# Linear attention: ScalarE weights the second expert rows, writes both norms and divides by the denominators; VectorE copies V with its bias

## The chip, the cores and the metric

The kernel runs on one core of a Trainium2 chip. Its time is device time in microseconds (us), the median of several executions: 1312.03 before the change, over 3 runs from 1311.81 to 1312.66. The core has a matrix engine (TensorE, PE in the profile, with its weight loads as PEld), three engines that work element by element (VectorE as DVE, ScalarE as ACT, GpSimd as POOL), and a queue that issues transfers (SyncE, SP). Each engine takes its instructions in the order in which they were written for it; semaphores order them against other engines.

## The reference

Six layers follow each other on x of 8 x 256 rows of 128 numbers: a feed-forward block with local attention, an attention with decay, the first block again, a mixture of experts, a linear attention, and the mixture of experts once more. The change is in the linear attention, and in how the experts' results before and behind it are added to x:

```
yr = sum over the two best experts of w[n] * expert(n)       # mixture: ys + yr
x = x + 0.5 * (ys + yr)
xn = (x - mean) * rsqrt(var + 1e-5) * ln_g + ln_b            # of x, itself layer-normed first
q, k, v = split(xn @ w_qkv + b_qkv)
k = k * sigmoid(xn @ w_gate + b_gate)
q, k = elu(q) + 1, elu(k) + 1
num = (q @ k.T * causal mask) @ v
den = sum(q * cumsum(k)) + 1e-6
x = x + num / den @ w_proj + b_proj
```

Behind it stands the norm of the next mixture of experts.

## The kernel before, in words

X holds all 2048 rows as 16 tiles of 128 x 128. The linear attention works in NCH = 4 chunks of CT = 4 tiles (512 rows, two sequences). There is no planner: each engine has a function (la_pe, la_act, la_dve, la_pool) in which the order of the work is written out by hand, and the engines meet at semaphores. The stage begins when the rows of the experts' results come back from memory: for each chunk one transfer into U (first expert) and one into uT (second expert), issued one after the other by SyncE (L2239). It ends with a barrier of all engines (phase_end), behind which the next mixture of experts picks its experts.

First half, by chunk c:
- VectorE, added(c): add_experts (L2149) adds weight times row for the first expert and then for the second, one scalar_tensor_tensor a tile, eight a chunk; moments (L2445, L2449) takes mean and variance. Then normed(c-1, 0) (L2455) writes (x - mean) * rs of the chunk before into U.
- GpSimd, power(c, 0) (L2548, L2550): rs = (a * var + b) to the power -1/2. Behind the four powers it adds the projection's bias to X (x_bias, L2555).
- TensorE, turned(c) (L2259): transposes the four tiles of U. ScalarE, normed(c) (L2382): copies the turned chunk to uT with the norm's gain and bias. TensorE, gate_proj(c) (L2266), k_proj, q_proj. ScalarE, gates(c) (L2387): the sigmoid.
- TensorE's written order there: turned(0), turned(1), gate_proj(0), k_proj(0), turned(2), gate_proj(1), q_proj(0), turned(3), gate_proj(2), gate_proj(3), v_proj(0). v_proj(0) waits for all four gates, since V and a gate share a bank.

Second half, a loop over i in which the engines are some chunks apart:
- ScalarE: o_out(i-1) (L2414) copies the turned output of chunk i-1 out of its bank; exps(i+1) (L2395 to L2401) for both feature maps; v_out(i+1) (L2407) copies V out; x_out(i-2) (L2418).
- VectorE: gated(i+1) (L2469), masked(i) (L2485), result(i-1) (L2511: adds the projected output to X, then takes the moments for the next norm), features(i+1) (L2474, L2477), divided(i) (L2492, L2498: the denominators; L2504: four tiles times 1/denominator into osb), normed(i-1, 1) (L2455 again, into U).
- GpSimd: v_bias(c) (L2560) adds V's bias in place; power(c, 1).
- TensorE: out_proj(i-1), x_turned(i-2) (L2332), sums(i) (waits for V with bias, and for x_new of chunk i-1, since the banks are used again), k_proj, v_proj, scores, q_proj, o_turn(i) (L2317), and at the end the logits of the next stage (L2339).

The last stage of the kernel (add_last on VectorE, scale_second on ScalarE, L2156, L2164, L2168) adds the experts' rows of the second mixture: ScalarE multiplies the second expert's rows by their weights in place, VectorE adds the first expert's rows tile by tile and the second's with one tensor_tensor for the whole chunk.

Of the kernel before, what the change touches and what calls it, by code (L numbers as in the profile page):

```python
# [126 lines left out]
def build(nc, a, out):  # L127
    with ExitStack() as ctx:
# [177 lines left out]
        ndr = sb("ndr", [P, 2, CT])  # L306

# [1824 lines left out]
        def sums(k0, c):  # L2132
            return 2 * NT + c * (CT + 1) if k0 else 2 * c * CT

        def wait_added(eng, k0, c):
            eng.wait_ge(s.x_sum, sums(k0, c) + (CT + 1 if k0 else 2 * CT))
# [4 lines left out]
        def add_experts(dve, k0, c):  # L2141

            dve.wait_ge((s.gat0, s.gat1, s.gat2, s.gat3)[c], 16 * 2 * (k0 + 1))
            dve.wait_ge(s.s_tmp, NCH * (k0 + 1))
            for n in range(2):
                for t in range(c * CT, (c + 1) * CT):
                    if n:
                        dve.wait_ge(s.x_sum, sums(k0, c) + t - c * CT + 1)
                    dve.scalar_tensor_tensor(X[:, t, :], gathered(n, c)[:, t - c * CT, :], wc[:, n, t:t + 1], X[:, t, :],  # L2149
                                             ALU.mult, ALU.add).then_inc(s.x_sum, 1)  # L2150

        def scale_second(act, c):
            act.wait_ge((s.gat0, s.gat1, s.gat2, s.gat3)[c], 16 * 4)
            for t in range(CT):
                g = gathered(1, c)[:, t, :]
                m = act.activation(g, g, ACT.Identity, scale=wc[:, 1, c * CT + t:c * CT + t + 1])  # L2156
            m.then_inc(s.x_scaled, 1)

        def add_last(dve, c):
            xc = X[:, c * CT:(c + 1) * CT, :]  # L2160
            dve.wait_ge((s.gat0, s.gat1, s.gat2, s.gat3)[c], 16 * 4)
            dve.wait_ge(s.s_tmp, NCH * 2)
# [3 lines left out]
            dve.wait_ge(s.x_scaled, c + 1)  # L2166
            dve.wait_ge(s.x_sum, sums(1, c) + CT)
# [85 lines left out]
        def la_pe(pe, ph):  # L2253
# [47 lines left out]
            def sums(c):  # L2301
                v_, w = vA[c % 2], D + 1
                pe.wait_ge(s.p_sum, NCH + c + 1)
# [75 lines left out]
        def la_act(act, ph):  # L2379
# [44 lines left out]
            normed(0)  # L2424
            for c in range(1, NCH):
                normed(c)
                gates(c - 1)
            gates(NCH - 1)
            act.preload_act_table(ACT.Exp)
            for i in range(-1, NCH + 2):  # L2430
                if has(i - 1):
                    o_out(i - 1)
                if has(i + 1):
                    exps(i + 1)
                    v_out(i + 1)
                if has(i - 2):
                    x_out(i - 2)
            phase_end(act, "act", ph)

        def la_dve(dve, ph):  # L2440
# [10 lines left out]

            def normed(c, k):
                dve.wait_ge(s.rs_ready, LA_RS + k * NCH + c + 1)
                for t in range(c * CT, (c + 1) * CT):
                    m = dve.tensor_scalar(U[:, t, :], X[:, t, :], mv[:, t, 0:1], rs[:, 1, t:t + 1],  # L2455
                                          ALU.subtract, ALU.mult)
                m.then_inc(s.ln_done, 1)
# [29 lines left out]
            def divided(c):  # L2487
# [174 lines left out]
```

## Time and profile before

| | |
|---|---|
| median of 3 runs | 1312.03 us |
| the profiled execution, own time | 1309.68 us |
| its span in the profile | 1307.8 us |
| PE busy | 1153.8 us, 88% |
| DVE busy | 915.5 us, 70% |
| ACT busy | 850.6 us, 65% |
| POOL busy | 789.2 us, 60% |
| mean granted TensorE clock | 0.961 of full speed |

Busy time is what an engine spends in instructions, added up over the span; it hides which engine is waited for at a given moment. The linear attention runs from 1077 us to some 1150 us of the span, 5 to 6% of it. In a timeline each row gives its start, its length, the engine, the source line, the operation, what it writes and reads, how many instructions were merged, and in brackets how long the engine had been idle and what ended that. X is the residual, U and uT the two buffers named above, mv the moments, rs the reciprocal deviations, osb (sm in the rows) the divided output.

### The profile page before, as it was taken

To read this page: it belongs to the slowest core of one execution; us is meant where nothing else is said; L and a number is where in the kernel's file an instruction comes from. 1 tells how busy PE (TensorE), PEld (TensorE's weight loads), DVE (VectorE), ACT (ScalarE), POOL (GpSimd) and SP (SyncE) were. 2 spreads that over 40 slices of the span, in tenths; PEclk is the share of its full clock that TensorE was granted. 3 is DMA by queue.
4 is the path that set the end of the run, shared out by engine and by line. 5 is a ranking of instruction groups with operands and counts; after the bars stand their busy time and mean duration, and the time that the engine had idled before them with its cause. 6 is when DMAs were issued, how large, how long until landed. Compare 5 with 4: busy or idle time off the path is not lost.

```text
span 1307.8 us, 36416 instructions
## 1 busy us (share of the span) xinstructions
PE 1153.8 (88%) x12703; PEld 865.5 (66%) x12704; DVE 915.5 (70%) x2475; ACT 850.6 (65%) x2476; POOL 789.2 (60%) x705
## 2 busy tenths in 40 slices
PE   5899898999888999979998989989979985779995
PEld 2576685777755666536766856768569873648985
DVE  6898678887765666769886698878754337774334
ACT  3899858999544455549998589994425543334554
POOL 5888438886456354168873488854377753237772
PEclk8999999999989999989999999999879996978998
DMA  7011100011000000000111000113157650025775
GB/s 222 22 25 28 29 9 20 22 27 26 21 11 3 4 3 3 3 1 18 26 26 29 17 10 22 26 26 93 45 143 220 202 157 26 1 81 160 230 199 154
DMA packets 69808, 78.21 MB, mean 60 GB/s; under 512 B 25094, under 2 KB 50501, under 8 KB 69509
## 3 DMA queue, kind: packets, MB, share of 16 engines
q1 hardware_dynamic: 64133, 64.70, 17.6%
q0 software_dynamic: 5504, 11.28, 3.5%
q8 instruction: 100, 1.64, 0.6%
q14 instruction: 71, 0.58, 0.2%
HBM read 54.60 MB, written 8.78 MB: 48 GB/s over the span
## 4 chain that ended last, share of the span: by engine, by line
PE 55%; DVE 12%; ACT 10%; DMA 8%; POOL 6%; issue 5%; POOLq 1%; SPq 1%; DVEq 0%; ACTq 0%
PE bank L916 5%; PE bank L1846 5%; ACT pB L795 4%; DMA arena<-arena 3%; PE bank L637 3%; PE bank L600 3%; DMA y_rows<-stg,inv_u 3%; PE bank L928 3%; PE bank L1515 3%; PE bank L559 3%; PE bank L545 3%; PE bank L612 3%; PE bank L1536 3%; PE bank L551 3%; POOL arena L2176 2%
## 5 line engine op out<-in xcount | busy, mean ns | idle before, releaser
L864 POOL TENSOR_TENSOR rn<-ss,mhalf 128x16 f32<-128x16 f32 x64 | 187.2, 2924 | 6.8
L2104 DVE SCALAR_TENSOR_TENSOR act_b<-bank,vec,gl 128x128 f32<-128x128 f32 x258 | 75.0, 345 | 133.0 <-ACT gl L1927 112.9
L1846 PE MATMUL bank<-arena 128*128 128x128 f32 x1032 | 135.5, 282 | 1.6 <-issue 1.6
L1846 PEld LDWEIGHTS bank<-arena 128*128 128x128 f32 x1032 | 126.1, 197 | 6.2 <-issue 5.3
L795 ACT ACTIVATE pA<-bank,nb,rn 128x128 f32<-128x128 f32 x256 | 113.5, 484 | 3.0 <-DVE nb L726 3.0
L795 ACT ACTIVATE pB<-bank,nb,rn 128x128 f32<-128x128 f32 x256 | 113.3, 478 | 1.7 <-DVE nb L726 1.7
L850 POOL TENSOR_TENSOR arena<-arena 128x512 f32<-128x512 f32 x64 | 81.5, 1274 | 46.0 <-DVE nb L726 34.9
L1927 ACT ACTIVATE gl<-bank,vec 128x128 f32<-128x128 f32 x258 | 76.0, 365 | 51.1 <-PE bank L1846 36.0
L857 POOL TENSOR_TENSOR arena<-arena 128x512 f32<-128x512 f32 x64 | 81.3, 1271 | 43.1 <-DVE arena L689 16.4
L1609 DVE TENSOR_REDUCE act_b<-bank 128x2 f32<-128x512 f32 x128 | 79.5, 684 | 39.6 <-PE bank L1491 39.6
L2182 POOL DMA_INDIRECT y_rows<-stg,inv_u x86 | 84.6, 983 | 35.0 <-issue 18.6
L2176 POOL DMA_INDIRECT arena<-u_rows,inv_u x86 | 84.0, 977 | 32.5 <-issue 22.5
L721 DVE TENSOR_REDUCE mx<-bank 128x4 f32<-128x512 f32 x128 | 82.4, 685 | 25.9 <-PE bank L600 25.9
L687 DVE TENSOR_TENSOR arena<-bank,arena 128x512 f32<-128x512 f32 x128 | 87.4, 683 | 13.9 <-ACT arena L762 12.8
L776 ACT ACTIVATE pT<-bank 128x512 f32<-128x512 f32 x128 | 77.2, 604 | 22.8 <-PE bank L612 19.8
L762 ACT ACTIVATE arena<-bank 128x512 f32<-128x512 f32 x128 | 78.3, 613 | 18.5 <-PE bank L545 9.5
L916 PE MATMUL bank<-hT,arena 128*128 128x256 f32 (+1 forms) x384 | 89.2, 382 | 0.0
L689 DVE TENSOR_TENSOR arena<-bank,arena 128x512 f32<-128x512 f32 x128 | 87.0, 680 | 0.0
L1079 POOL TENSOR_SCALAR rs<-mv 128x2 f32<-128x2 f32 x48 | 10.9, 226 | 125.6 <-DVE mv L978 125.6
L784 ACT ACTIVATE arena<-bank 128x512 f32<-128x512 f32 x128 | 78.6, 614 | 8.0 <-PE bank L567 4.8
L637 PE MATMUL bank<-pT,arena 128*64 128x64 f32 (+1 forms) x1536 | 71.9, 242 | 13.5 <-DMA arena<-arena 12.0
L1052 ACT ACTIVATE gl<-bank,vec 128x256 f32<-128x256 f32 (+1 forms) x96 | 45.3, 472 | 49.6 <-PE bank L916 49.2
(334 smaller groups left out, 3135.9 us busy)
## 6 DMA issues: line engine op xcount, KB each, us to landing
arena<-in_L_ffn_We SPq DMA_DIRECT2D x86, 384.0 KB, 4.3
arena<-arena SPq DMA_DIRECT2D x64, 128.0 KB, 2.3
arena<-in_L_ffn_We SPq DMA_DIRECT2D x3, 768.0 KB, 7.4
arena<-U SPq DMA_DIRECT2D x32, 64.0 KB
u_rows<-U SPq DMA_DIRECT2D x2, 1024.0 KB, 5.2
U<-y_rows SPq DMA_DIRECT2D x8, 256.0 KB, 4.2
uT<-y_rows SPq DMA_DIRECT2D x8, 256.0 KB, 4.7
arena<-U SPq DMA_DIRECT2D x32, 63.5 KB
```

Of the source, the lines that this page charges most:

```text
L637: m = pe.matmul(BO[64 * x:64 * x + 64, cols], v[:, h * LD:(h + 1) * LD], pT[x][:, cols], start=True, stop=True)
L687: dve.tensor_tensor(heads(rab[:, 2 * k, :]), heads(bank[:, :]), bc(rtab[:, l, 2 * k, q % 2, :].unsqueeze(1), [P, LH, LD]), ALU.mult)
L689: dve.tensor_tensor(rab[:, 2 * k + 1, :].rearrange("p (h a d) -> p h a d", h=LH, a=2), flipped(bank[:, :]), bc(rtab[:, l, 2 * k + 1, q % 2 ...
L721: dve.tensor_reduce(mx8[:, par, x, :], BS[x][:, :].rearrange("p (u k) -> p u k", u=4), AX_X, ALU.max, negate=True)\
L795: m = act.activation(pr[:, u * P:(u + 1) * P], BS[x][:, u * P:(u + 1) * P], ACT.Exp, bias=nb8[:, par, x, u:u + 1], scale=rn[:, q % 4, 0, 2 ...
L850: pool.tensor_tensor(kadd[:, :], rab[:, 2, :], rab[:, 3, :], ALU.add).then_inc(s.kadd_ready, 1)
L857: pool.tensor_tensor(qr[:, :], rab[:, 0, :], rab[:, 1, :], ALU.add).then_inc(s.qr_ready, 1)
L864: pool.tensor_tensor(rn[:, q % 4, :, :], ss[:, 1, :].rearrange("p (a h) -> p a h", a=2), mhalf[:, :].rearrange("p (a h) -> p a h", a=2), A ...
L916: m = pe.matmul(MG[c][0:n, g * SEQ:(g + 1) * SEQ], w1[:, g * HID + h0:g * HID + h0 + n], hT2[:, :], start=True, stop=True)
L1846: m = pe.matmul(bank[q % 2][:, j * P:(j + 1) * P], we1[q][:, half * HR + j * P:half * HR + (j + 1) * P], xT[:, q, :], start=True, stop=True)
L2176: pool.indirect_dma_start(xg[:, n % XG, :], None, u_rows[:, :], bass.IndirectOffsetOnAxis(ap=inv_u[:, 0, n:n + 1], axis=0))\
L2182: pool.indirect_dma_start(y_rows[:, :], bass.IndirectOffsetOnAxis(ap=inv_u[:, 1, n:n + 1], axis=0), yb[:, n % 4, :], None)\
```

## The change

ScalarE takes over from VectorE: the weighting of the second expert's rows ahead of the linear attention (scale_second now serves both places; add_last becomes add_experts for both), the norms (x_normed, with a bias of -mean * rs that GpSimd computes into the new tile nmr), and the division by the denominators (divided; VectorE keeps inverted). VectorE takes over v_out from ScalarE and adds V's bias in it; GpSimd's v_bias goes. ScalarE's loop over the first half is now by steps of three chunks apart. TensorE's list stays, but for the semaphore of V.

```diff
-        def add_experts(dve, k0, c):
-            dve.wait_ge((s.gat0, s.gat1, s.gat2, s.gat3)[c], 16 * 2 * (k0 + 1))
-            dve.wait_ge(s.s_tmp, NCH * (k0 + 1))
-            for n in range(2):
-                for t in range(c * CT, (c + 1) * CT):
-                    if n:
-                        dve.wait_ge(s.x_sum, sums(k0, c) + t - c * CT + 1)
-                    dve.scalar_tensor_tensor(X[:, t, :], gathered(n, c)[:, t - c * CT, :], wc[:, n, t:t + 1], X[:, t, :],
-                                             ALU.mult, ALU.add).then_inc(s.x_sum, 1)
-        def scale_second(act, c):
-            act.wait_ge((s.gat0, s.gat1, s.gat2, s.gat3)[c], 16 * 4)
+        def scale_second(act, k0, c):
+            act.wait_ge((s.gat0, s.gat1, s.gat2, s.gat3)[c], 16 * 2 * (k0 + 1))
             for t in range(CT):
                 g = gathered(1, c)[:, t, :]
                 m = act.activation(g, g, ACT.Identity, scale=wc[:, 1, c * CT + t:c * CT + t + 1])
             m.then_inc(s.x_scaled, 1)
-        def add_last(dve, c):
+        def add_experts(dve, k0, c):
...
             for t in range(CT):
                 dve.scalar_tensor_tensor(xc[:, t, :], gathered(0, c)[:, t, :], wc[:, 0, c * CT + t:c * CT + t + 1],
                                          xc[:, t, :], ALU.mult, ALU.add).then_inc(s.x_sum, 1)
-            dve.wait_ge(s.x_scaled, c + 1)
+            dve.wait_ge(s.x_scaled, k0 * NCH + c + 1)
...
             dve.tensor_tensor(xc, xc, gathered(1, c), ALU.add).then_inc(s.x_sum, 1)
@@ la_pe, sums
-                pe.wait_ge(s.p_sum, NCH + c + 1)
+                pe.wait_ge(s.n_v, c + 1)
@@ la_act
-            def v_out(c):
-                act.wait_ge(s.n_vps, c + 1)
-                if c > 1:
-                    act.wait_ge(s.n_num, 2 * c - 2)
-                act.activation(vA[c % 2][:, :, 0:D], LB_V[:, :].rearrange("p (t d) -> p t d", t=CT), ACT.Copy)\
-                    .then_inc(s.n_v, 1)
+            def x_normed(c, k):
+                act.wait_ge(s.rs_ready, LA_RS + k * NCH + c + 1)
+                for t in range(c * CT, (c + 1) * CT):
+                    m = act.activation(U[:, t, :], X[:, t, :], ACT.Identity, bias=nmr[:, 1, t:t + 1],
+                                       scale=rs[:, 1, t:t + 1])
+                m.then_inc(s.ln_done, 1)
+            def divided(c):
+                act.wait_ge(s.n_rec, c + 1)
+                if c:
+                    act.wait_ge(s.n_oT_ps, c)
+                for j in range(CT):
+                    o0 = (j % 2) * (D + 1)
+                    m = act.activation(osb[:, j, :], LB_N[j // 2][:, o0:o0 + D], ACT.Copy, scale=ndr[:, 1, j:j + 1])
+                m.then_inc(s.n_o, 1)
...
-            normed(0)
-            for c in range(1, NCH):
-                normed(c)
-                gates(c - 1)
-            gates(NCH - 1)
+            for c in range(NCH + 2):
+                if has(c):
+                    scale_second(act, 0, c)
+                if has(c - 1):
+                    x_normed(c - 1, 0)
+                if has(c - 2):
+                    normed(c - 2)
+                    gates(c - 2)
             act.preload_act_table(ACT.Exp)
             for i in range(-1, NCH + 2):
                 if has(i - 1):
                     o_out(i - 1)
                 if has(i + 1):
                     exps(i + 1)
-                    v_out(i + 1)
                 if has(i - 2):
                     x_out(i - 2)
+                if has(i):
+                    divided(i)
+                if has(i - 1):
+                    x_normed(i - 1, 1)
@@ la_dve
-            def normed(c, k):
...
-                for j in range(CT):
-                    o0 = (j % 2) * (D + 1)
-                    m = dve.tensor_scalar(osb[:, j, :], LB_N[j // 2][:, o0:o0 + D], ndr[:, 1, j:j + 1], None, ALU.mult)
-                m.then_inc(s.n_o, 1)
+            def v_out(c):
+                dve.wait_ge(s.n_vps, c + 1)
+                if c > 1:
+                    dve.wait_ge(s.n_num, 2 * c - 2)
+                dve.tensor_tensor(vA[c % 2][:, :, 0:D], LB_V[:, :].rearrange("p (t d) -> p t d", t=CT),
+                                  bc(lbv_row[:, :].unsqueeze(1), [P, CT, D]), ALU.add).then_inc(s.n_v, 1)
...
-            added(0)
-            for c in range(1, NCH):
+            for c in range(NCH):
                 added(c)
-                normed(c - 1, 0)
-            normed(NCH - 1, 0)
...
                 if has(i):
-                    divided(i)
-                if has(i - 1):
-                    normed(i - 1, 1)
+                    inverted(i)
+                if has(i + 1):
+                    v_out(i + 1)
@@ la_pool, power
-                pool.tensor_scalar(rs[:, 0, ts], mv[:, ts, 1], a_, b_, ALU.mult, ALU.add).then_inc(s.p_self, 1)
+                pool.tensor_scalar(rs[:, 0, ts], mv[:, ts, 1], a_, b_, ALU.mult, ALU.add)
+                pool.tensor_scalar(nmr[:, 0, ts], mv[:, ts, 0], -1.0, 0.0, ALU.mult, ALU.add).then_inc(s.p_self, 1)
                 pool.wait_ge(s.p_self, next(p_own))
-                pool.tensor_tensor(rs[:, 1, ts], rs[:, 0, ts], mhalf[:, 0:CT], ALU.pow).then_inc(s.rs_ready, 1)
+                pool.tensor_tensor(rs[:, 1, ts], rs[:, 0, ts], mhalf[:, 0:CT], ALU.pow).then_inc(s.p_self, 1)
+                pool.wait_ge(s.p_self, next(p_own))
+                pool.tensor_tensor(nmr[:, 1, ts], nmr[:, 0, ts], rs[:, 1, ts], ALU.mult).then_inc(s.rs_ready, 1)
...
-            v_bias(0)
             for c in range(NCH):
-                if c + 1 < NCH:
-                    v_bias(c + 1)
                 power(c, 1)
```

## Rows read from the trace of the kernel before

**Rows 1.** Busy time by engine in two stretches: start:end, length, then each engine.
```profile
1077.00:1104.00 27.00, 12.22 (x34) 6.22 (x35) 21.10 (x81) 7.16 (x10) 9.79 (x12) 0.66 0.19 51
1104.00:1131.00 27.00, 23.45 (x139) 17.95 (x139) 20.55 (x61) 12.88 (x23) 7.80 (x8) 0.96 0.00 1
```

**Rows 2.** Timeline of VectorE, first half: start, length, engine, line, operation.
```profile
1077.12 1.14 DVE L2149 SCALAR_TENSOR_TENSOR X<-U,wc,X 128x128 f32<-128x128 f32 x4 [1.51 <-DMA uT<-y_rows]
...
1079.35 0.87 DVE L2445 BATCH_NORM_STATS2 st<-X 128x6 f32<-128x128 f32 x4
1080.25 0.38 DVE L2449 BATCH_NORM_AGGREGATE mv<-st 128x2 f32<-128x6 f32 x4
1080.55 1.10 DVE L2149 SCALAR_TENSOR_TENSOR X<-U,wc,X 128x128 f32<-128x128 f32 x4
...
1083.94 1.08 DVE L2455 TENSOR_SCALAR U<-X,mv,rs 128x128 f32<-128x128 f32 x4
...
1094.27 3.98 DVE L2455 TENSOR_SCALAR U<-X,mv,rs 128x128 f32<-128x128 f32 x4 [0.41 <-POOL rs L2550]
```

**Rows 3.** Timeline of TensorE, first half.
```profile
1089.50 1.11 PE L2259 MATMUL bank<-ident_sb,U 128*128 128x128 f32 x4 [3.31 <-DVE U L2455]
1090.41 1.91 PE L2266 MATMUL bank<-uT,ngate 128*128 128x512 f32 x2
...
1094.42 1.02 PE L2266 MATMUL bank<-uT,ngate 128*128 128x512 f32 x2
```

**Rows 4.** Timeline of ScalarE, first half: the sigmoids.
```profile
1092.36 0.69 ACT L2387 ACTIVATE arena<-bank,vec 128x512 f32<-128x512 f32 x1 [0.93 <-PE bank L2266]
...
1095.48 0.69 ACT L2387 ACTIVATE arena<-bank,vec 128x512 f32<-128x512 f32 x1
...
1101.98 0.69 ACT L2387 ACTIVATE arena<-bank,vec 128x512 f32<-128x512 f32 x1 [1.02 <-PE bank L2266]
```

**Rows 5.** Timeline of all engines, second half.
```profile
1129.53 1.13 DVE L2504 TENSOR_SCALAR sm<-bank,ndr 128x128 f32<-128x128 f32 x4
...
1131.41 0.60 ACT L2414 ACTIVATE pT<-bank 128x512 f32<-128x512 f32 x1 [1.12 <-PE bank L2317]
...
1138.01 0.60 ACT L2414 ACTIVATE pT<-bank 128x512 f32<-128x512 f32 x1 [3.73 <-PE bank L2317]
...
1139.93 0.69 DVE L2511 TENSOR_TENSOR X<-bank,X 128x512 f32<-128x512 f32 x1 [1.64 <-PE bank L2323]
...
1143.34 1.11 DVE L2455 TENSOR_SCALAR U<-X,mv,rs 128x128 f32<-128x128 f32 x4 [1.41 <-POOL rs L2550]
```

**Rows 6.** Timeline of GpSimd, last chunk's power.
```profile
1142.02 0.19 POOL L2548 TENSOR_SCALAR rs<-mv 128x4 f32<-128x4 f32 x1 [5.30 <-DVE mv L2449]
1142.30 1.01 POOL L2550 TENSOR_TENSOR rs<-rs,mhalf 128x4 f32<-128x4 f32 x1
```

**Rows 7.** Timeline of ScalarE and VectorE at the kernel's end.
```profile
1297.04 1.28 ACT L2156 ACTIVATE uT<-uT,wc 128x128 f32<-128x128 f32 x4 [7.42 <-DMA uT<-y_rows]
...
1303.15 1.13 DVE L2164 SCALAR_TENSOR_TENSOR X<-U,wc,X 128x128 f32<-128x128 f32 x4
1304.39 0.69 DVE L2168 TENSOR_TENSOR X<-X,uT 128x512 f32<-128x512 f32 x1
```

**Rows 8.** Groups by line and shape: busy, mean ns of one, idle before.
```profile
L795 ACT ACTIVATE pA<-bank,nb,rn 128x128 f32<-128x128 f32 x256 | 113.5, 484 | 3.0 <-DVE nb L726 3.0
...
L1927 ACT ACTIVATE gl<-bank,vec 128x128 f32<-128x128 f32 x258 | 76.0, 365 | 51.1 <-PE bank L1846 36.0 <-issue 13.4 <-DVE act_b L2104 1.6
...
L1934 ACT ACTIVATE stg<-bank 128x128 f32<-128x128 f32 x86 | 23.9, 277 | 48.2 <-DMA y_rows<-stg,inv_u 36.3 <-PE bank L1860 11.4
...
L2156 ACT ACTIVATE uT<-uT,wc 128x128 f32<-128x128 f32 x16 | 5.1, 390 | 9.3 <-DMA uT<-y_rows 9.3
```

**Rows 9.** Busy time by microsecond; third number from the end is the granted clock.
```profile
1092.00:1093.00 1.00, 1.00 (x3) 0.34 (x1) 0.96 (x8) 0.64 (x1) 0.05 (x1) 0.77 0.00 0
...
1099.00:1100.00 1.00, 1.00 (x2) 0.17 (x1) 0.00 (x0) 0.78 (x1) 0.60 (x1) 0.65 0.00 0
```

More of the change, by code:

```diff
@@ L306, in build @@
         ndr = sb("ndr", [P, 2, CT])
+        nmr = sb("nmr", [P, 2, NT])
         u_rows = nc.dram_tensor("u_rows", [NT * P, D], F32, kind="Internal").ap()
@@ L2132, in sums @@
         def sums(k0, c):
-            return 2 * NT + c * (CT + 1) if k0 else 2 * c * CT
+            return (k0 * NCH + c) * (CT + 1)
         def wait_added(eng, k0, c):
-            eng.wait_ge(s.x_sum, sums(k0, c) + (CT + 1 if k0 else 2 * CT))
+            eng.wait_ge(s.x_sum, sums(k0, c) + CT + 1)
         def gathered(n, c):
             return (U[:, :, :], uT[:, :].rearrange("p (t d) -> p t d", d=D))[n][:, c * CT:(c + 1) * CT, :]
-        def add_experts(dve, k0, c):
-            dve.wait_ge((s.gat0, s.gat1, s.gat2, s.gat3)[c], 16 * 2 * (k0 + 1))
-            dve.wait_ge(s.s_tmp, NCH * (k0 + 1))
-            for n in range(2):
-                for t in range(c * CT, (c + 1) * CT):
-                    if n:
-                        dve.wait_ge(s.x_sum, sums(k0, c) + t - c * CT + 1)
-                    dve.scalar_tensor_tensor(X[:, t, :], gathered(n, c)[:, t - c * CT, :], wc[:, n, t:t + 1], X[:, t, :],
-                                             ALU.mult, ALU.add).then_inc(s.x_sum, 1)
-        def scale_second(act, c):
-            act.wait_ge((s.gat0, s.gat1, s.gat2, s.gat3)[c], 16 * 4)
+        def scale_second(act, k0, c):
+            act.wait_ge((s.gat0, s.gat1, s.gat2, s.gat3)[c], 16 * 2 * (k0 + 1))
             for t in range(CT):
@@ L2157, in scale_second @@
             m.then_inc(s.x_scaled, 1)
-        def add_last(dve, c):
+        def add_experts(dve, k0, c):
             xc = X[:, c * CT:(c + 1) * CT, :]
-            dve.wait_ge((s.gat0, s.gat1, s.gat2, s.gat3)[c], 16 * 4)
-            dve.wait_ge(s.s_tmp, NCH * 2)
+            dve.wait_ge((s.gat0, s.gat1, s.gat2, s.gat3)[c], 16 * 2 * (k0 + 1))
+            dve.wait_ge(s.s_tmp, NCH * (k0 + 1))
             for t in range(CT):
@@ L2165, in add_last @@
                                          xc[:, t, :], ALU.mult, ALU.add).then_inc(s.x_sum, 1)
-            dve.wait_ge(s.x_scaled, c + 1)
-            dve.wait_ge(s.x_sum, sums(1, c) + CT)
+            dve.wait_ge(s.x_scaled, k0 * NCH + c + 1)
+            dve.wait_ge(s.x_sum, sums(k0, c) + CT)
             dve.tensor_tensor(xc, xc, gathered(1, c), ALU.add).then_inc(s.x_sum, 1)
@@ L2450, in moments @@
                 m.then_inc(s.stats_ready, 1)
-            def normed(c, k):
[L2453 to L2457, printed above, removed]
             def added(c):
@@ L2485, in masked, with inverted @@
                     dve.tensor_tensor(am[b][:, :], LB_A[b][:, 0:384], causal[:, :], ALU.mult).then_inc(s.n_am, 1)
-            def divided(c):
+            def inverted(c):
                 for b in range(2):
@@ L2555, in x_bias @@
                 pool.tensor_tensor(xc, xc, bc(lbp_row[:, :].unsqueeze(1), [P, CT, D]), ALU.add).then_inc(s.p_sum, 1)
-            def v_bias(c):
-                v_ = vA[c % 2][:, :, 0:D]
-                pool.wait_ge(s.n_v, c + 1)
-                pool.tensor_tensor(v_, v_, bc(lbv_row[:, :].unsqueeze(1), [P, CT, D]), ALU.add).then_inc(s.p_sum, 1)
             for c in range(NCH):
@@ L2575, in fin_dve @@
             for c in range(NCH):
-                add_last(dve, c)
+                add_experts(dve, 1, c)
         def fin_sync(sp):
@@ L2613, in _ @@
             for c in range(NCH):
-                scale_second(act, c)
+                scale_second(act, 1, c)
         @block.vector
```

3 lines of the change are left out of this document (removed).

## The prediction

> **What bounds the kernel now.** I read the page first, for size: VectorE is busy 70% of the span and ScalarE 65%. The diff touches the linear attention stage and renames the pieces of the last additions, so I cut the span there: from 1077.1 us, when the gathered rows of chunk 0 have landed, to 1151, when the next stage starts. In the first 27 us VectorE is busy 21.1 and ScalarE 7.2; in the next 27 it is TensorE with 23.5 [rows 1]. So there are two halves with two limits, and I read each in the timelines and in the chain of waits.
>
> First half (chunks are added, normalised, turned, gated). VectorE runs without a break: a chunk takes 2.23 us of additions (1077.12 to 1079.35), 1.20 of moments to the start of what comes next (1080.55) and 1.0 to 1.1 of norm, 4.4 in all. The last norm takes 3.98, while GpSimd adds a bias to X in the same microseconds [rows 2]. When it ends (1098.25), four gate steps alternate between TensorE and ScalarE; the last sigmoid starts at 1101.98 and ends at 1102.67 [rows 3, 4], and a table load and the exponentials hang on that.
>
> Second half (a loop over four chunks). The chain goes through TensorE, the short copy of the turned output by ScalarE (o_out, L2414), the output projection, VectorE's result, and TensorE again [rows 5]. VectorE's copy-outs, divisions and norms lie beside that until the end. There the last norm stands alone in the chain: moments 1141.56, GpSimd's two operations 1142.02 to 1143.31, norm 1143.34 to 1144.45 [rows 5, 6], then the last turn.
>
> **The change, part by part.** The profiled execution took 1309.7 us, of which the span is 1307.8; the median of the runs is 1312.0. I work out a shift against the trace and add it to the median.
>
> *Additions.* A chunk's eight scalar_tensor_tensors become four, and one tensor_tensor of the whole chunk. The tail of this kernel has just this form: the four start 1.23 us ahead of the tensor_tensor, and that takes 0.69 (1303.15, 1304.39) [rows 7]. With the moments (0.03 to their start, then 0.90 and 0.30 from start to start [rows 2]) VectorE needs 1.24 + 0.69 + 0.03 + 1.20 = 3.16 us a chunk. ScalarE's four weightings take 1.28 beside them [rows 7].
>
> *Norm on ScalarE.* One such activation, from SBUF with a scale per row, takes 0.390; it lets the next start 0.09 earlier. The norm has a bias per row too. That form from SBUF is not in the trace. An activation with a bias per row takes 0.365 against 0.277 for a plain copy, so 0.09 for each operand [rows 8]: I take 0.48, and four in 3 x 0.39 + 0.48 = 1.63 us. Bounds: 1.28 (nothing for the second operand) and 1.9 (4 x 0.484, the exponentials with two such operands, with no overlap) [rows 8]. On VectorE it was 1.11 [rows 5].
> A page speaks against this move: the Trainium skill (ScalarE: Activation LUTs, Rules for kernel authors) gives adds and multiplies to VectorE and not to ScalarE. The rows agree, 1.63 us against 1.11; by the rule alone the change would lose 0.5 us wherever a norm stands on the path and nothing elsewhere, which is the least part of the sum below.
>
> *GpSimd.* The pair takes 1.30 us from start to release (0.28, then 1.01) [rows 6]. Two operations on 4 columns are added: a tensor_scalar and, behind a wait, a product. The tensor_scalar of that size takes 0.19; with 0.1 of wait I take 0.50 for both, bounds 0.2 and 1.3 (the product as slow as the power). So a chunk's norm may start 0.48 + 1.80 = 2.28 us after its bn_aggr starts.
>
> *Sum of the first half: the order of ScalarE's queue.* Its new loop holds, for c = 2: weighting(2), norm(1), normed(0), gates(0), and only then weighting(3). gates(0) waits for a matmul that stands in TensorE's queue behind turned(1), so behind norm(1). The steps, in us:
> - Chunk 0: bn_aggr at 1080.05 (1077.12, then 1.31 to the tensor_tensor, which ScalarE's 1.28 holds up here, and 0.69 + 0.03 + 0.90). Its norm on ScalarE 1082.37 to 1084.0, behind weighting(1). Weighting(2) to 1085.2. Norm(1), free at 1080.05 + 3.16 + 2.28 = 1085.5, runs to 1087.2; normed(0) to 1087.9.
> - turned(1) starts 1087.2 and the gate matmul 0.91 later (as 1089.50, 1090.41 [rows 3]); the sigmoid starts 1.95 after it (1090.41, 1092.36) [rows 3, 4]: 1090.1. ScalarE stands still 2.2 us, and weighting(3) waits behind it: 1090.7 to 1092.0.
> - So chunk 3's tensor_tensor is at 1092.0 although VectorE was ready at 1088.1; bn_aggr 1.62 later, the norm's numbers at 1093.6 + 2.28 = 1095.9, against 1094.24 before.
> - ScalarE: norm(2) to 1093.5, normed(1) to 1094.2, gates(1) at 1094.5 + 1.95 = 1096.4, to 1097.1; norm(3) to 1098.7 (before: 1098.25); normed(2) to 1099.35. Only then can gate matmul 2 start: 1099.6, gates(2) 1101.6 to 1102.3, normed(3) to 1103.0, matmul 3, gates(3) 1104.95 to 1105.65. Before: 1102.67. **+3.0.** That normed(2), which now stands behind norm(3), is no longer done in advance costs most of the last part.
>
> This takes 1.95 us from matmul to sigmoid, which is the trace's step at a granted clock of 0.50 (1.2 GHz); at 1.00 it is 1.06 (1094.42, 1095.48) [rows 3, 4]. The clock is at the low level when the stage's first turns run; it comes back at about 1092.5, after TensorE had worked from 1089.5 on, and falls again at about 1099.4 after the idle time 1096.3 to 1098.3 [rows 3, 9]. After the change TensorE works in shorter pieces (1087.2 to 1091.5, 1093.6 to 1098, 1098.7 to 1101.6), so I take the low level. If it came back for the last two gates the same sum gives 2 x 0.9 less: +1.2. With only the first gate slow it is about 0.
>
> *Second half.* VectorE's copy of V (a tensor_tensor from a bank, 0.69 as L2511 [rows 5]) stands after the denominators. v_proj(1) to (3) are done there by then, and the bias additions by GpSimd that go were never waited for: nothing. The denominators' division moves to ScalarE: four copies with a scale per row, about 0.26 apart and 0.36 long, 1.14 against 1.13 [rows 5, 8]: nothing. But in ScalarE's queue norm(i-1) now follows divided(i) and stands ahead of o_out(i), which is on the chain:
> - i = 1: division 1120.85, norm(0) to 1123.5; o_out(1) starts 1123.99: hidden, by 0.4 us.
> - i = 2: division 1129.53, norm(1) 1130.56 to 1132.2, so o_out(2) at 1132.1 against 1131.41 [rows 5]: +0.7. No other work is between; projection, result and sums(3) move with it.
> - i = 3: division 1136.8, norm(2) 1137.9 to 1139.6, o_out(3) 1139.5 against 1138.01 [rows 5]: +0.8 more.
> - Last norm: +0.5 on GpSimd [rows 6] and +0.5 on ScalarE (1.63 against 1.11). These have no cover; the turn, the logits and the barrier follow.
> Together **+2.5** (bounds 1.0 with all the low ends, 4 with all the high).
>
> *Last stage.* The same instructions under other names: nothing. Sum: +5.5 us, **1312.0 + 5.5 = 1317.5 us**.
>
> **Rivals.**
> 1. The clock returns earlier in the first half: +1.2 + 2.5 = 3.7, 1315.7; with nearly all gates fast, 2.5, 1314.5. For it: the rows between 1092.5 and 1099.4 do have 1.00, and the places are near each other. Against: ScalarE's queue now spaces TensorE's work out.
> 2. Faster: VectorE is the engine of the first half, and taking 1.24 us a chunk plus the norm of 3.98 off it is what counts. It decides if ScalarE stands still for the gates under 0.5 us in all: bn_aggr(3) then is at 1080.05 + 3 x 3.16 = 1089.5, norm(3) ends at 1093.5, and the gates after it at about 1098, 4.5 earlier. With the second half as worked out: 1312 - 4.5 + 2.5 = 1310.0; with that half's losses hidden too 1307.5. For it: the 21.1 us against 7.2 of [rows 1]. Against: gates(0) cannot start before turned(1), whatever the clock.
> 3. The halves cancel: the first gains 1 to 3 (all clocks high, two-operand activations at 1.28), the second loses 2: 1311 to 1313, no change.
> 4. More than forecast: the next stage starts later at the low clock too, or the product on GpSimd takes 1 us: 1319 to 1321.
>
> **How the numbers follow.** Forecast 0.52, rival 1 0.25, rival 2 0.06, rival 3 0.09, rival 4 0.08. What can be told from no change is 0.2%, 2.6 us: slower are the forecast, rival 4 and most of rival 1: 0.80. Same: the rest of rival 1 and rival 3, 0.14. Faster: 0.06. The range, 1313.5 to 1319.8, holds the forecast with its bounds and rival 1.
>
> **What would show it.** In the first half: a gap of about 2 us on ScalarE ahead of the first sigmoid, the last tensor_tensor of VectorE some 4 us after its scalar_tensor_tensors, the last sigmoid ending 3 us later than 1102.67. In the second: o_out(2) and o_out(3) starting right behind a norm and not behind TensorE; four norms of 1.6 us; the last GpSimd group 1.8 long. I am wrong if ScalarE's first sigmoid waits for nothing, if the granted clock is 1.00 from about 1092 on, or if o_out stays behind TensorE.

## The result and the profile after

The changed kernel takes 1317.26 us in the median of 10 runs (1314.25 to 1321.89), the kernel before 1311.92 in 10 runs beside it (1308.56 to 1313.57): a ratio of 1.0043, interval 1.0027 to 1.0058, slower. The profiled execution took 1320.8 us with a span of 1318.9. That is 11.1 over the profiled execution of before, but 6.9 of it lie ahead of the stage, in code that the diff leaves alone: the rows of chunk 0 land at 1084.04 instead of 1077.12. So from here on I count from that landing, inside each trace. As the landing I take the start of VectorE's first addition.

Busy time by engine in the two stretches that answer to [rows 1], after:

```profile
1084.00:1111.00 27.00, 12.78 (x32) 5.67 (x33) 12.62 (x53) 17.24 (x41) 11.86 (x20) 0.68 0.18 49
1111.00:1138.00 27.00, 21.86 (x127) 16.83 (x126) 15.96 (x44) 15.06 (x32) 2.49 (x5) 0.94 0.00 1
```

VectorE's 21.1 us have become 12.6 and ScalarE's 7.2 have become 17.2: the work moved as planned, and the stretch did not get shorter.

Timeline of ScalarE, first half, after:

```profile
1092.99 1.65 ACT L2396 ACTIVATE U<-X,nmr,rs 128x128 f32<-128x128 f32 x4 [0.82 <-POOL nmr L2548]
1094.54 0.76 ACT L2372 ACTIVATE uT<-bank,vec 128x512 f32<-128x512 f32 x1
1097.55 0.69 ACT L2377 ACTIVATE arena<-bank,vec 128x512 f32<-128x512 f32 x1 [2.25 <-PE bank L2256]
1098.13 1.26 ACT L2146 ACTIVATE uT<-uT,wc 128x128 f32<-128x128 f32 x4
1099.30 1.63 ACT L2396 ACTIVATE U<-X,nmr,rs 128x128 f32<-128x128 f32 x4
...
1107.15 0.69 ACT L2377 ACTIVATE arena<-bank,vec 128x512 f32<-128x512 f32 x1 [1.22 <-PE bank L2256]
1107.74 0.77 ACT L2372 ACTIVATE uT<-bank,vec 128x512 f32<-128x512 f32 x1
1109.72 0.69 ACT L2377 ACTIVATE arena<-bank,vec 128x512 f32<-128x512 f32 x1 [1.22 <-PE bank L2256]
```

The first sigmoid waits 2.25 us for its product, and weighting(3), at 1098.13, stands behind it. The four gate products of TensorE, after, and the second sigmoid, which is left out above:

```profile
1095.60 1.91 PE L2256 MATMUL bank<-uT,ngate 128*128 128x512 f32 x2
1101.65 1.35 PE L2256 MATMUL bank<-uT,ngate 128*128 128x512 f32 x2
1106.04 1.07 PE L2256 MATMUL bank<-uT,ngate 128*128 128x512 f32 x2
1108.56 1.12 PE L2256 MATMUL bank<-uT,ngate 128*128 128x512 f32 x2 [1.45 <-ACT uT L2372]
...
1103.05 0.69 ACT L2377 ACTIVATE arena<-bank,vec 128x512 f32<-128x512 f32 x1 [1.45 <-PE bank L2256]
```

From the start of a gate product to the start of its sigmoid it is 1.95, 1.40, 1.11 and 1.16 us; only the first runs wholly at the low clock. The last sigmoid ends 26.37 us after the landing (25.55 before [rows 4]). VectorE shows the other side: it is ready at 1095.2 and waits 4.19 us.

```profile
1094.13 1.11 DVE L2154 SCALAR_TENSOR_TENSOR X<-U,wc,X 128x128 f32<-128x128 f32 x4
1099.43 0.69 DVE L2158 TENSOR_TENSOR X<-X,uT 128x512 f32<-128x512 f32 x1 [4.19 <-ACT uT L2146]
```

Timeline of ScalarE in the loop of the second half, after; compare [rows 5]:

```profile
1138.95 1.14 ACT L2406 ACTIVATE sm<-bank,ndr 128x128 f32<-128x128 f32 x4 [2.33 <-DVE ndr L2496]
1139.97 1.65 ACT L2396 ACTIVATE U<-X,nmr,rs 128x128 f32<-128x128 f32 x4
1141.51 0.60 ACT L2413 ACTIVATE pT<-bank 128x512 f32<-128x512 f32 x1
...
1146.23 1.14 ACT L2406 ACTIVATE sm<-bank,ndr 128x128 f32<-128x128 f32 x4 [1.85 <-DVE ndr L2496]
1147.37 1.65 ACT L2396 ACTIVATE U<-X,nmr,rs 128x128 f32<-128x128 f32 x4
1148.92 0.57 ACT L2413 ACTIVATE pT<-bank 128x512 f32<-128x512 f32 x1
```

Both o_outs (L2413) come without an idle time, right behind a norm; before, they waited for TensorE. GpSimd's last group, after; compare [rows 6]:

```profile
1153.26 0.19 POOL L2543 TENSOR_SCALAR rs<-mv 128x4 f32<-128x4 f32 x1 [5.92 <-DVE mv L2454]
1153.51 0.19 POOL L2544 TENSOR_SCALAR nmr<-mv 128x4 f32<-128x4 f32 x1
1153.79 1.01 POOL L2546 TENSOR_TENSOR rs<-rs,mhalf 128x4 f32<-128x4 f32 x1
1154.87 0.20 POOL L2548 TENSOR_TENSOR nmr<-nmr,rs 128x4 f32<-128x4 f32 x1
```

And on ScalarE the norm that it releases:

```profile
1155.11 1.65 ACT L2396 ACTIVATE U<-X,nmr,rs 128x128 f32<-128x128 f32 x4 [2.57 <-POOL nmr L2548]
```

1.85 us from the first operation to the norm's start instead of 1.32, and 1.65 for the norm instead of 1.11. From the landing to the end of that norm it is 72.72 us instead of 67.33.

Not all of these 5.39 us reach the next stage. Its first instruction on VectorE, before and then after:

```profile
1150.66 0.36 DVE L2002 TENSOR_TENSOR pA<-bank,br_row 128x192 f32<-128x192 f32 x1 [6.21 <-POOLq L319]
1162.43 0.36 DVE L2003 TENSOR_TENSOR pA<-bank,br_row 128x192 f32<-128x192 f32 x1 [9.26 <-POOLq L320]
```

It is released by GpSimd's queue at the barrier, and it starts 7.35 us after the end of GpSimd's last instruction (1143.31) before the change and 7.36 after it (1155.07). The same distance, 7.35 or 7.36, stands in 13 of the 14 traces of this document (7.72 in e11), whether the last norm is on VectorE (1.11) or on ScalarE (1.65). TensorE, which works on what the norm wrote, has ended 1.81 us earlier in the first case and 1.28 in the second. So the 0.54 us that the norm takes longer are covered by the barrier, and from the landing to the next stage it is 78.39 us instead of 73.54: 4.85 more. What GpSimd's queue does in the 7.35 us no trace shows.

### The profile page after: what moved, and what is told of

It reads as the page before. It is cut to its first block, busy times and chain, and to the rows that moved or that the text cites. A ratio compares the mean times of both kernels' runs of the same rounds, so it can differ in the third digit from the quotient of the medians.

```text
span 1318.9 us, 36436 instructions
## 1 busy us (share of the span) xinstructions
PE 1163.2 (88%) x12703; PEld 871.4 (66%) x12704; DVE 900.6 (68%) x2419; ACT 870.5 (66%) x2536; POOL 788.4 (60%) x717
## 3 DMA queue, kind: packets, MB, share of 16 engines
q8 instruction: 100, 1.64, 0.5%
## 4 chain that ended last, share of the span: by engine, by line
PE 55%; ACT 11%; DVE 11%; DMA 9%; POOL 6%; issue 5%; SPq 1%; POOLq 1%; ACTq 0%; DVEq 0%
PE bank L1847 5%; PE bank L917 5%; ACT pB L796 5%; DMA arena<-arena 4%; PE bank L638 3%; PE bank L601 3%; PE bank L1516 3%; PE bank L560 3%; PE bank L929 3%; DMA y_rows<-stg,inv_u 3%; PE bank L546 3%; PE bank L1537 3%; PE bank L552 3%; PE bank L613 3%; PE bank L1861 2%
## 5 line engine op out<-in xcount | busy, mean ns | idle before, releaser
L777 ACT ACTIVATE pT<-bank 128x512 f32<-128x512 f32 x128 | 77.2, 603 | 24.8 <-PE bank L613 21.8
```

## The experiments

Each was timed in 12 runs beside 34 or 35 of the kernel before. A single execution varies by 3 us and more on either side, so a time tells one part of this change poorly. The traces, cut at the same events, separate the parts; but each is one execution with its own course of the clock. All numbers of the table are read from timelines: "sigmoid" is the end of the last sigmoid after the landing, scores(0) its first product, sums(n) the first product of L2309 (L2299 after) for chunk n, "norm" the end of the last norm, "next" the start of the next stage on VectorE. From sums(1) to sums(2) it is 8.68 us in every trace.

| kernel | sigmoid | scores(0) | scores(0) to sums(1) | sums(2) to sums(3) | sums(3) to norm | landing to norm | landing to next | ratio (interval) |
|---|---|---|---|---|---|---|---|---|
| before | 25.55 | 30.02 | 10.88 | 7.42 | 10.33 | 67.33 | 73.54 | |
| changed | 26.37 | 30.85 | 12.54 | 8.10 | 12.55 | 72.72 | 78.39 | 1.0043 (1.0027 to 1.0058) |
| e1 changed again | 26.75 | 31.22 | 12.55 | 8.10 | 13.12 | 73.67 | 79.34 | 1.0039 (1.0020 to 1.0058) |
| e2 first half only | 26.33 | 30.80 | 12.55 | 7.42 | 10.35 | 69.80 | 76.00 | 1.0024 (1.0005 to 1.0044) |
| e3 second half only | 24.57 | 29.04 | 12.56 | 8.09 | 12.98 | 71.35 | 77.03 | 1.0033 (1.0014 to 1.0052) |
| e4 weighting ahead | 24.44 | 28.91 | 10.88 | 8.09 | 13.08 | 69.64 | 75.32 | 1.0049 (1.0030 to 1.0067) |
| e5 norm behind o_out | 27.09 | 31.56 | 10.88 | 7.44 | 11.42 | 69.98 | 75.65 | 1.0021 (1.0006 to 1.0036) |
| e6 changed, filler | 25.12 | 30.42 | 10.77 | 8.09 | 13.12 | 71.08 | 76.75 | 1.0014 (1.0000 to 1.0028) |
| e7 before, filler | 24.57 | 29.04 | 10.88 | 7.42 | 10.41 | 66.43 | 72.63 | 0.9987 (0.9969 to 1.0005) |
| e8 reordered | 20.48 | 24.95 | 12.55 | 7.42 | 10.34 | 63.94 | 70.15 | 0.9967 (0.9953 to 0.9981) |
| e9 and TensorE's list | 20.14 | 24.61 | 12.55 | 7.41 | 10.34 | 63.59 | 69.80 | 0.9963 (0.9946 to 0.9980) |
| e10 copy and division | 24.56 | 29.03 | 10.88 | 7.43 | 10.35 | 66.37 | 72.57 | 0.9990 (0.9974 to 1.0006) |
| e11 weighting only | 24.56 | 29.03 | 10.88 | 7.42 | 10.33 | 66.34 | 72.92 | 0.9988 (0.9972 to 1.0004) |
| e12 reordered again | 20.25 | 24.72 | 12.56 | 7.41 | 10.35 | 63.72 | 69.92 | 0.9981 (0.9966 to 0.9997) |

**e1, the changed kernel again.**

> The changed kernel once more, as a second look at how the shift divides. I compare stretches inside the trace: A from the landing of chunk 0 to the start of scores(0), 30.0 us before, 30.9 in the first trace of the change; B from there to the end of the last norm, 37.3 before, 41.9. Theory (queue order, with the granted clock deciding in which half the slow matmuls fall): A between 30.5 and 33.5, B between 40 and 42, the sum 72 to 73.5 in every trace although the parts move against each other. Rival (the two halves have fixed costs of their own, 0.8 and 4.6): A 30.9 and B 41.9 again within 0.2.

The first stretch is 31.22, as expected, the second 42.45 and the sum 73.67, both above what either theory gave. The slowdown repeats, 1.0039. Two places differ from the first trace: the second gate waits 1.82 us for its product instead of 1.45, and the output projection of chunk 3 falls deeper into a low stretch of the clock. TensorE's timeline, first in the trace of the changed kernel above:

```profile
1149.55 1.50 PE L2313 MATMUL bank<-nproj,pT 128*128 128x128 f32 x8 [0.66 <-ACT pT L2413]
```

and then in e1:

```profile
1144.65 2.08 PE L2313 MATMUL bank<-nproj,pT 128*128 128x128 f32 x8 [0.67 <-ACT pT L2413]
```

Before the change it takes 1.16. Now it starts 5.34 us after the start of sums(3) instead of 4.54, and the clock has fallen by then or falls in it. It takes 1.50 to 2.08 in the five traces that have a norm ahead of o_out(3) on ScalarE (after, e1, e3, e4, e6) and 1.16 to 1.22 in the nine others.

**e2 and e3, one half each.** e2 takes the second half from the kernel before, e3 the first. Cut from ScalarE's loops and shortened, against the changed kernel:

```diff
 e2, la_act                           e3, la_act
-    divided(i); x_normed(i - 1, 1)   -    scale_second(act, 0, c); x_normed(c - 1, 0)
+    v_out(i + 1)                     +    normed(c); gates(c - 1)
```

> Only the first half of the change: additions with ScalarE's weighting and norm(c) on ScalarE with its bias from GpSimd; the second half (divisions and norms on VectorE, V's copy on ScalarE, V's bias on GpSimd) as before. Theory: the first half costs 1 to 3 us and the second is as it was, so 1 to 3 us over the kernel before, B at 37.3 to 38.8 (up to 1.5 for a clock that falls at its start), o_out(2) right behind TensorE. Rival (VectorE's relief in the first half is a gain that the second half spoils): 2 us or more faster than before.

> Only the second half of the change: divisions and norms on ScalarE, V's copy with bias on VectorE; the first half as before. Theory: B longer by what the queue costs, 0.7 at o_out(2), 0.8 at o_out(3), 0.5 on GpSimd and 0.5 for the last norm: A 30.0 as before, B about 39.8 to 40.2, the time 2.5 to 3 us over the kernel before. Rival (the first trace's 4.6 us are all the second half's own): B 41.9, 4.6 over.

Both are slower than before, by 3.1 and 4.3 us by their ratios, so neither half carried a gain, and the rival of e2 falls. e2's second half is as before but for 1.67 us between scores(0) and sums(1); e3 has the same 1.68 there, although its code there is another. Its B is 42.31 and not 39.8 to 40.2: the number lies nearer to the rival's 41.9. But 1.68 of it stands in e2 too, whose second half is the old one, and 0.78 is a projection of 1.94 us at the low clock; without the two B is 39.85. What e3 shows of ScalarE's queue alone is 8.09 against 7.42, and 12.98 less the 0.78 of the projection against 10.33: 2.5 together, the forecast.

The 1.67 is the clock. Busy time by microsecond, after; the third number from the end is the granted clock:

```profile
1115.00:1116.00 1.00, 1.00 (x6) 0.92 (x7) 1.00 (x2) 0.00 (x0) 0.00 (x0) 1.00 0.00 0
1116.00:1117.00 1.00, 1.00 (x5) 0.81 (x4) 0.81 (x3) 0.63 (x1) 0.00 (x0) 0.54 0.00 0
1117.00:1118.00 1.00, 1.00 (x2) 0.33 (x1) 0.30 (x1) 0.00 (x0) 0.00 (x0) 0.50 0.00 0
```

And on TensorE, scores(0) and q_proj(1):

```profile
1114.89 0.70 PE L2287 MATMUL bank<-pA 128*128 128x256 f32 x2 [2.40 <-DVE pA L2475]
...
1116.50 1.91 PE L2266 MATMUL bank<-uT,nqkv 128*128 128x512 f32 x2
```

TensorE had 2.40 us without work ahead of scores(0), and the granted clock falls from 1.00 to 0.50 (1.2 GHz) at about 1116.1, inside scores(0); q_proj(1) takes 1.91 us instead of 1.02. In the trace that I predicted from, the low stretch lay earlier, over the last gates [rows 9], and the products ahead of scores(0) were slow and filled that wait: 0.77 us of it was left. All seven traces with the 12.55 (after, e1, e2, e3, e8, e9, e12) have the wait of 2.40; of the seven with 10.77 to 10.88, six have at most 1.11, and one, e10, has 2.40 too and keeps its clock. So the fall follows such a wait, but not each time, and neither half's code decides: e2 and e5 have the changed first half, e3 and e10 the old one, and each pair shows both lengths.

**e4, weighting(3) ahead of the gates.** The loop of ScalarE's first half, shortened:

```diff
+    scale_second(act, 0, 0)
     for c in range(NCH + 2):
-        if has(c): scale_second(act, 0, c)
+        if has(c + 1): scale_second(act, 0, c + 1)
```

> The changed kernel with each weighting one step earlier in ScalarE's queue, so that weighting(3) stands ahead of gates(0). VectorE's last tensor_tensor then waits for nothing and its last moments end some 4 us earlier. Theory: those moments were not what the first half waited for; ScalarE's own queue of norms, turns and gates is, and it only loses 1.2 us of work behind gates(0): A shorter by 1 to 1.5 us than in the changed kernel. Rival (the late moments of chunk 3 are on the path): A shorter by 3 to 4 us, and the kernel about as fast as before.

VectorE no longer waits; its last bn_aggr starts at 12.36 us after the landing instead of 17.02, 4.7 earlier. The sigmoid is 1.9 to 2.3 earlier, not 4: the late moments were mostly hidden. The size was above my 1 to 1.5: against the first trace of the changed kernel it is 0.53 from an earlier gates(0), 1.17 from the weighting that no longer stands behind it, and 0.23 from a second gate that is wholly at the high clock. The times do not show the gain: 1.0049, with an interval that overlaps that of the changed kernel. The profiled execution, 1311.95 us, is one of the fastest of its 12 runs (median 1316.06), so this trace does not stand for them; why most of them are slower stays open. One trace is what speaks for the gain.

**e5, the norm behind the next o_out.** The loop of ScalarE's second half, shortened:

```diff
     if has(i - 1): o_out(i - 1)
+    if has(i - 2): x_normed(i - 2, 1)
...
     if has(i): divided(i)
-    if has(i - 1): x_normed(i - 1, 1)
```

> The changed kernel with the second half's norm(i-2) placed behind o_out(i-1) in ScalarE's queue instead of norm(i-1) ahead of it. Theory: what the second half loses inside the loop is ScalarE's queue order: o_out(2) and o_out(3) again start right behind TensorE's turn, from sums(2) to sums(3) 7.4 us as before the change (8.1 with it), and from sums(3) to the end of the last norm 11.3 to 11.8 instead of 12.6 to 13.1, since only GpSimd's 0.5 and the norm's 0.5 stay. In all 1.4 us off. Rival (the loop's loss is ScalarE's longer division or VectorE's copy of V): 8.1 and 12.6 stay.

7.44 and 11.42: as expected. ScalarE in this kernel, at chunk 3:

```profile
1142.59 1.14 ACT L2406 ACTIVATE sm<-bank,ndr 128x128 f32<-128x128 f32 x4 [1.26 <-DVE ndr L2496]
1144.48 0.60 ACT L2413 ACTIVATE pT<-bank 128x512 f32<-128x512 f32 x1 [0.75 <-PE bank L2307]
1144.97 1.64 ACT L2396 ACTIVATE U<-X,nmr,rs 128x128 f32<-128x128 f32 x4
```

o_out waits for TensorE again. The 1.09 over the 10.33 of before are GpSimd's 0.53 and the norm's 0.54, and the latter is covered by the barrier: from scores(0) to the next stage it is 44.09 us, 0.57 over the 43.52 of before. The projection is at the high clock here too, so one move of a call gave back the queue's 1.5 and, in this trace, the clock's share behind it. The ratio, 1.0021, is below that of the changed kernel, with intervals that overlap.

**e6 and e7, the clock held by filler.** Both add products to TensorE's list into a bank that nothing uses there. The list, shortened (only the filler is new):

```diff
+    filler(10); turned(0); filler(3); turned(1); gate_proj(0); k_proj(0); filler(2); turned(2)
+    gate_proj(1); q_proj(0); filler(1); turned(3)    # and filler(2) ahead of scores(0)
```

> The changed kernel with extra products on TensorE into a bank that is free there: 10 ahead of turned(0), 3 ahead of turned(1), 2 ahead of turned(2), 1 ahead of turned(3), 2 ahead of scores(0), each 128x512, 0.86 us at the high clock. They add work that the reference doesn't have and change no output. They keep the granted clock at 1.00 through the first half. Theory: with every gate step at 1.06 us the first half of the changed kernel ends its last sigmoid at 24.2 to 24.8 us after the landing of chunk 0 (26.4 and 26.8 without), and the sum from landing to the last norm is 70 to 70.8. Rival (the first half's length is ScalarE's queue alone, not the clock): 26.4 stays.

> The kernel before with the same 18 extra products at the same places of TensorE's list. Theory: its last sigmoid ends at 24.2 to 24.7 (25.6 without), so with the clock taken out the first half costs 0 to 0.5 us more after the change than before it, and the second half the rest, 2.9 to 3.5: landing to last norm 66.5 to 67 here against 70 to 70.8. Rival (the change's first half is slower at any clock by ScalarE's queue): its last sigmoid 1.5 us or more ahead of that of the changed kernel with filler.

The granted clock is 1.00 from 4 us after the landing to the last sigmoid in both. The sigmoid ends at 25.12 after the change (24.8 at most was expected) and 24.57 before it: at the high clock the changed first half costs 0.55 us, a little more than I wrote. The remaining 1.2 to 2.0 us of the four traces without filler go with the low clock. The 71.08 of e6 is above 70.8; in it are 0.83 us of the filler itself ahead of scores(0). By their ratios the two differ by 0.27%, 3.5 us. e7 is not told from the kernel before.

**e8 and e12, ScalarE's queue written anew, the second half as before.** The order, in short:

```diff
-    for c in range(NCH + 2): ...
+    scale 0, scale 1, scale 2, norm 0, scale 3, norm 1, normed 0, norm 2, normed 1,
+    gates 0, norm 3, normed 2, gates 1, normed 3, gates 2, gates 3
```

> A version meant to beat both: the first half of the change with ScalarE's queue written as weighting 0, 1, 2, norm 0, weighting 3, norm 1, normed 0, norm 2, normed 1, gates 0, norm 3, normed 2, gates 1, normed 3, gates 2, gates 3, and the second half as before the change. Theory: VectorE is never held up, norm(3) ends at 16.4 to 17 us after the landing (21.1 before), the last sigmoid at 21 to 23 (25.6), the second half as before: 3 us faster than the kernel before, ratio 0.998. Rival (TensorE's list, with k_proj(0) and q_proj(0) between the turns at the low clock, becomes the limit): last sigmoid at 24 or later, no gain.

> The reordered version (e8) once more, for its time on another run and a second trace. Theory: last sigmoid at 20 to 21 us after the landing, landing to last norm 62.5 to 64.5 (67.3 before), ratio 0.996 to 0.998. Rival (e8's time was luck of one chip): ratio not below 0.999.

This beats both kernels: 0.9967 and 0.9981, both intervals below 1. The last sigmoid is 5 us earlier than before, at 20.48 and 20.25. ScalarE, e8, from norm(2) on:

```profile
1089.79 1.65 ACT L2403 ACTIVATE U<-X,nmr,rs 128x128 f32<-128x128 f32 x4 [0.83 <-POOL nmr L2563]
1091.34 0.76 ACT L2372 ACTIVATE uT<-bank,vec 128x512 f32<-128x512 f32 x1
1092.00 0.67 ACT L2377 ACTIVATE arena<-bank,vec 128x512 f32<-128x512 f32 x1
1092.91 1.65 ACT L2403 ACTIVATE U<-X,nmr,rs 128x128 f32<-128x128 f32 x4 [0.24 <-POOL nmr L2563]
```

The first sigmoid (1092.00) waits for nothing, the norms wait for GpSimd and so for VectorE, which is never held up. It is the same work as in e2; only the order of ScalarE's queue differs. Between their sigmoids (26.33 and 20.48) lie 5.85 us, 6.08 with e12: so much the order is worth, together with the course of the clock that comes with it.

Part of what e8 gains on the kernel before has to do with GpSimd. Beside its addition of the projection's bias the last norm on VectorE took 3.98 us instead of 1.08 [rows 2]. The addition, before, and then the norm on ScalarE beside it, after:

```profile
1094.20 3.71 POOL L2555 TENSOR_TENSOR X<-X,lbp_row 128x512 f32<-128x512 f32 x3
...
1103.63 1.64 ACT L2396 ACTIVATE U<-X,nmr,rs 128x128 f32<-128x128 f32 x4
1103.30 4.93 POOL L2553 TENSOR_TENSOR X<-X,lbp_row 128x512 f32<-128x512 f32 x4
```

VectorE's single norm takes 0.31 to 0.35 us alone and up to 1.30 beside the addition; ScalarE's four take 1.64 beside it and 1.65 without it. From the start of the last bn_aggr to the end of the last norm it is 5.77 us before and 3.97 in e8, so 1.8 of e8's 5.1 us are this, and 3.0 are the last bn_aggr, which starts at 12.36 instead of 15.36.

**e9, TensorE's list too.** The list, shortened, without the filler:

```diff
-    gate_proj(0); k_proj(0); turned(2); gate_proj(1); q_proj(0); turned(3); gate_proj(2); gate_proj(3)
+    gate_proj(0); turned(2); gate_proj(1); k_proj(0); turned(3); gate_proj(2); gate_proj(3); q_proj(0)
```

> The reordered version (e8) with TensorE's list changed too: k_proj(0) behind gate_proj(1), q_proj(0) behind gate_proj(3), and 12 extra products (10 ahead of turned(0), 2 ahead of turned(1)) that only hold the granted clock. Theory: the wait for the first sigmoid, which in e8 starts 13.8 us after the landing, is the clock and the list; it starts 1 us earlier and the last sigmoid ends at 19.0 to 19.8 instead of 20.5: 0.7 to 1.5 us off e8. Rival (norm(3), at 14.7 to 16.4, and three dependent steps behind it set the end): 20.3 to 20.7, no gain.

20.14, 0.1 to 0.3 below e12 and e8. The first sigmoid starts at 13.77 as in e8, and not 1 us earlier, although the clock is at 1.00 up to the last sigmoid. So the theory falls and the number is next to the rival's 20.3 to 20.7: norm(3), which ends at 16.33, and the steps behind it set the end. Its ratio is not told from theirs.

**e10 and e11, single parts in the kernel before.** Cut from ScalarE's part:

```diff
 e10, la_act                 e11, la_act
-    v_out(i + 1)            +    for c in range(NCH): scale_second(act, 0, c)
+    divided(i)                   normed(0)
```

> The kernel before with two parts of the change alone: the division by the denominators on ScalarE and V's copy with its bias on VectorE, GpSimd's bias of V gone; all norms and additions as before. Theory: both lie beside the chain: sums(2) to sums(3) 7.4 us, sums(3) to the last norm 10.3 to 10.6, the time within 1 us of the kernel before. Rival (VectorE's copy, which stands between the denominators and gated or masked, or the longer ScalarE queue, delays the loop): sums(1) to sums(2) above 8.7 or sums(3) to norm above 10.8.

> The kernel before with one part of the change alone: ScalarE weights the second expert's rows (all four weightings first in its queue), VectorE adds them with one tensor_tensor a chunk; the norms stay on VectorE. Theory: VectorE still is the limit of the first half and gains 0.25 us a chunk: bn_aggr of chunk 3 starts at 14.5 to 14.8 us after the landing (15.4 before), the kernel 0.5 to 1 us faster, not to be told from no change. Rival (the additions are what ScalarE's help is worth, the norm is not): the same gain as the reordered version, bn_aggr(3) near 12.4.

e10: every stretch of the second half as before. The division on ScalarE and the copy on VectorE cost and bring nothing. e11: the last bn_aggr starts at 14.41 (15.36 before), and the last turn (L2248, L2259 in e10) at 20.23 for 21.18. Yet the sigmoid ends at 24.56 in both, since in e11 the low clock fell on the last two gates. TensorE's timeline, e11:

```profile
1100.12 3.10 PE L2255 MATMUL bank<-uT,ngate 128*128 128x512 f32 x4
```

and e10:

```profile
1099.45 2.16 PE L2266 MATMUL bank<-uT,ngate 128*128 128x512 f32 x4
```

The weighting alone is worth 0.95 us at the last bn_aggr, and the clock took 0.94 of it in this trace. The last norm is still on VectorE, beside GpSimd, with 3.98 us. The rest of e8's gain comes only with the norm off VectorE: its bn_aggr is another 2.05 us earlier.

## Why the prediction was right, point by point

The time (1317.26 for 1317.5) and the sum from landing to the last norm (+5.4 for +5.5) came out. The two halves did not: +0.8 and +4.6 in the first trace, for +3.0 and +2.5. The order of the queue was understood, but that the time agrees to 0.3 us is luck: 2.2 us that were forecast at the low clock in the first half did not come, 2.0 us at the low clock came in the second half, where none were forecast, and the barrier gave back 0.5 of a term.

- *Durations.* Additions: the bn_aggrs of chunks 1 and 2 follow after 3.14 and 3.72 us (the latter chunk waits 0.68 for weighting(2)), 3.16 forecast. Norm 1.65 for 1.63, division 1.14 for 1.14, GpSimd +0.53 for +0.50. Right.
- *Order in the first half.* The stall of 2.2 us ahead of gates(0) is there with 2.25, weighting(3) behind it, and VectorE's wait of 4.2. The mechanism was right. Mis-sized is the step of 1.95 us from product to sigmoid, taken for every gate: it measured 1.95, 1.40, 1.11 and 1.16, which is 2.2 less in all, and the sigmoid ended 26.4 us after the landing instead of 28.5. The clock came back before the third turn; it fell once more, mostly over q_proj(0) and the last turn. That is near rival 1, which gave +1.2.
- *What it was compared with.* Three further traces with the old first half (e3, e7, e10) end their sigmoid at 24.6; the one that I predicted from had its last gates at the low clock and 25.55. Against 24.6 the first half of the changed kernel, 26.3 to 27.1 in four traces (the changed kernel twice, e2, e5), is 1.8 to 2.5 slower. 0.55 of it stays at the high clock (e6, e7).
- *Second half, inside the loop.* The queue's two steps are there with 0.68 and 0.82 for 0.7 and 0.8, and e5 takes them away by moving one call.
- *Second half, last norm.* GpSimd's 0.53 and ScalarE's 0.54 are there for 0.5 each. Of the second I wrote that it has no cover. It has: the next stage waits for GpSimd's queue, 7.35 us behind GpSimd's last instruction, with a norm of 1.11 us as with one of 1.65. This term reaches the next stage with 0.0.
- *Second half, left out.* Two places at the low clock were not in the sum: 1.66 between scores(0) and sums(1), which is no cost of the second half's code, since it stands in e2 and e8 as well, and 0.35 to 0.9 in the projection of chunk 3.
- *Nothing* for copy and division: e10. The last stage, from the first addition to the end of the last, takes 8.04 us before and 8.23 after; e10, which has it unchanged, takes 8.54. No cost can be told.
- *Rivals.* Rival 2 (VectorE's relief counts) gave its condition, under 0.5 us of standing still for gates. The change does not meet it. e8 does (its sigmoids wait 0.45 us in all), and there the price was right: 4.5 us forecast, 5.1 measured at the sigmoid against the trace that I predicted from, 4.1 against the three at 24.6. Rival 4 added the next stage: after the change it runs at the low clock until 1167, but from its first instruction on VectorE to GpSimd's comparisons (L2186, L2196 before) it takes 15.43 us, 15.34 before: nothing.
- *The Trainium skill* (ScalarE: Activation LUTs, Rules for kernel authors) gives adds and multiplies to VectorE and not to ScalarE. The traces agree on the price where nothing else runs, 1.65 us against 1.11. It was the small part: at the last norm the barrier covers it, and ahead of the gates ScalarE's 1.64 beside GpSimd's addition is cheaper than VectorE's 3.98.

Not settled: how much of a single execution's spread, 6 us and more between runs of one kernel, comes from where the clock falls. The traces show 1.67 us for one such place; the stretch ahead of the stage alone differed by 6.9 between two traces. The profiled execution of the changed kernel, 1320.8 us, lies 3.5 above the median of its runs, so the shift of a single trace and that of the medians agree only roughly: 4.85 and 5.8 us to the next stage in the two traces of the changed kernel, 5.3 in the medians.

## What to carry to other kernels

When work moves to an idle engine, read its new queue line by line: each instruction that waits holds up all behind it, and work placed behind such a wait can cost all that the move brings; here the same work in another order went from 0.24% slower to 0.2 or 0.3% faster. Ask what covers a longer last step: at a barrier only the engine that arrives last counts. A trace holds one course of the clock: add queue waits from it, but ask for each product whether its duration is at the high or the low level, and compare several traces before a half is given a price.

## What was not expected of the hardware

- A fall of the clock behind scores(0) came in one size: from scores(0) to sums(1) 14 traces show 10.77 to 10.88 us or 12.54 to 12.56 and nothing between. The same 2.40 us without products was followed by a fall in seven traces and by none in e10, whose clock had come back latest, between 17 and 18 us after the landing.
- The filler brought nothing that can be told to the kernel before: with 1.00 granted from 4 to 61 us after the landing, e7 ends its sigmoid at 24.57, and so do e3 and e10 without filler, whose low stretches lay where TensorE had slack.
- In 13 of 14 traces the stage behind the barrier started 7.35 or 7.36 us after GpSimd's last instruction, one on 128x4 numbers; TensorE's last product had ended 1.28 us or more before that start.
- VectorE's norm of 128x128 numbers took 0.31 to 0.35 us alone and up to 1.30 beside an addition of 128x512 on GpSimd, and ScalarE's was not slowed by the same addition.
